# Windowed attention in six layers on one core: the roots of Q move from GpSimd's products into ScalarE's exponentials, in 64-key pieces

## The reference

```
q = l2norm(q) * qs;  k = l2norm(k) * ksc
q = q * cos * scale + rotate_half(q) * sin * scale
k = k * cos / scale + rotate_half(k) * sin / scale
sim = einsum('bhwie,bhwje->bhwij', bq, bk2) * 8      # 32 queries, 64 keys
sim = where(mask, -max, sim)                         # a key is visible 32 back
out = einsum('bhwij,bhwje->bhwie', softmax(sim, -1), bv2)
x = x + out @ Wo
x = x + (a * gelu(gate)) @ W2 + b2                   # a, gate = norm(x) @ W1 + b1
```

## Time and profile before

| | us |
|---|---|
| median of three runs | 4397.81 (4393.16 to 4399.85) |
| profiled execution | 4392.85 |
| its span, first to last instruction | 4391.0 |
| TensorE matmuls, busy | 3735.3 (85%) |
| VectorE busy | 2756.5 (63%) |
| GpSimd busy | 2491.9 (57%) |
| ScalarE busy | 1823.6 (42%) |
| mean granted clock of TensorE | 0.934 of full |

### The profile page before, as it was taken

The page is one execution under the profiler, slowest core; times in us unless marked ns, Lnnn a source line. Parts: engine busy times, 40 slices in busy tenths (PEclk is TensorE's granted clock), DMA queues, the critical chain, the costliest instruction groups (busy, mean ns, idle before and its releaser), DMA issues.

```text
span 4391.0 us, 146256 instructions
## 1 busy us (share of the span) xinstructions
PE 3735.3 (85%) x65128; PEld 2403.2 (55%) x65320; DVE 2756.5 (63%) x3583; ACT 1823.6 (42%) x2989; POOL 2491.9 (57%) x1948
## 2 busy tenths in 40 slices
PE   8999986788888888888888888888888888888887
PEld 4444443455555555556555555555555555555554
DVE  4544553666666666667677666666766666666662
ACT  4545553333443434344344343434344434343333
POOL 0000001866677766767667676666766667666651
PEclk9999997898999999999999999998999999999897
DMA  1000001544444444444444444444444444444331
GB/s 43 6 6 6 8 3 34 160 134 128 134 139 141 138 132 127 144 133 146 132 137 143 129 138 134 131 132 130 150 131 138 129 128 134 138 132 138 125 115 41
DMA packets 222595, 490.18 MB, mean 112 GB/s; under 512 B 63759, under 2 KB 101901, under 8 KB 221837
## 3 DMA queue, kind: packets, MB, share of 16 engines
q1 hardware_dynamic: 196080, 465.08, 33.8%
q10 hardware_dynamic: 25884, 15.73, 1.3%
HBM read 224.80 MB, written 7.34 MB: 53 GB/s over the span
## 4 chain that ended last, share of the span: by engine, by line
PE 52%; DVE 13%; issue 13%; POOL 9%; ACT 8%; DMA 3%; SPq 1%; ACTq 0%; DVEq 0%; POOLq 0%
PE PS L518 52%; ACT AOT L1235 2%; POOL SC L1338 2%; DVE TPB L924 2%; ACT SX L1212 2%; POOL Q L1315 2%; DVE MX L950 2%; POOL K L1315 2%; DVE PX L970 1%; ACT SC L1229 1%; DMA TR<-TPB 1%; DVE SC L952 1%; DMA PP<-PX 1%; POOL Q L1333 1%; DVE PP L969 1%
## 5 line engine op out<-in xcount | busy, mean ns | idle before, releaser
L924 DVE SCALAR_TENSOR_TENSOR TPB<-PS,VEC,C 128x1024 f32<-128x1024 f32 x768 | 977.7, 1282 | 590.8 <-ACT SX L1212 555.1
L518 PE MATMUL PS<-PP,VV 32*64 32x64 f32 (+1 forms) x24576 | 572.0, 229 | 253.7 <-ACT AOT L1235 149.0
L518 PEld LDWEIGHTS PS<-PP,VV 32*64 32x64 f32 x24576 | 461.6, 138 | 528.4 <-issue 484.5
L1338 POOL TENSOR_TENSOR SC<-SC,RC 128x1024 f32<-128x1024 f32 x192 | 365.7, 1904 | 543.7 <-DVE RC L961 543.7
L1315 POOL TENSOR_TENSOR Q<-Q,RB 128x512 f32<-128x512 f32 x384 | 491.2, 1279 | 134.9 <-DMA RB<-root_scratch 134.1
L1212 ACT ACTIVATE SX<-PS 128x512 f32<-128x512 f32 x768 | 460.5, 601 | 233.1 <-PE PS L518 227.8
L1333 POOL TENSOR_TENSOR Q<-TPB,TR 128x512 f32<-128x512 f32 x384 | 489.5, 1275 | 118.1 <-DMA TR<-TPB 103.4
L1315 POOL TENSOR_TENSOR K<-K,RB 128x512 f32<-128x512 f32 x384 | 491.3, 1280 | 0.0
L1333 POOL TENSOR_TENSOR K<-TPB,TR 128x512 f32<-128x512 f32 x384 | 490.0, 1276 | 0.0
L1225 ACT COPY VV<-PS 128x512 f32<-128x512 f32 x384 | 223.2, 581 | 625.4 <-PE PS L518 575.6
L518 PE MATMUL PS<-LXH,LH 128*128 128x512 f32 x768 | 362.3, 472 | 13.2 <-POOL LL L1309 8.0
(11 more groups left out here) (164 smaller groups left out, 6644.9 us busy)
## 6 DMA issues: line engine op xcount, KB each, us to landing
TR<-TPB SPq DMA_DIRECT2D x768, 256.0 KB
RB<-root_scratch SPq DMA_DIRECT2D x768, 256.0 KB, 4.1
PP<-PX SPq DMA_DIRECT2D x192, 192.0 KB, 3.0
WS<-in_wqkv ACTq DMA_DIRECT2D x72, 128.0 KB, 2.5
PP<-PX SPq DMA_DIRECT2D x192, 48.0 KB, 4.0
root_scratch<-NV SPq DMA_DIRECT2D x384, 8.0 KB
LO<-in_wo ACTq DMA_DIRECT2D x6, 512.0 KB, 5.2
T<-in_x SPq DMA_DIRECT2D x8, 256.0 KB, 3.1
```

Source lines behind the costliest of these rows:

```text
L518: return e.matmul(dst, lhsT, rhs, start=start, stop=stop, **kw)
L924: e.scalar_tensor_tensor(TPB[:, n % 3:4 + n % 2:3 + n % 2 - n % 3, w, :], g, VEC[:, l, 9 + w:10 + w], C[:, at:at + 1024].rearrange("p (o c ...
L1338: e.tensor_tensor(sc, sc, RC[m % 2][:, :].rearrange("p (g o) -> p g o", o=1).broadcast_to([128, 16, 64]), ALU.mult).then_inc(sem["np_pool" ...
```

## The change

The roots of Q are no longer multiplied into Q. The scores in banks 0 and 1 so lack a factor for each query and head, and ScalarE applies it: exp(r * score - r * MX), with r from a small tile RQ as scale and -MX * r from a small tile BQ as bias. Both are one number per partition, so one exponential covers one group of 64 keys, 16 of them for a pair, straight from PSUM. The subtraction on VectorE goes; a product of 128x16 makes BQ. RQ, once in four rounds, is a transpose on TensorE of NV and a copy on ScalarE. The selection matrix tsel orders the rows so that the 8 roots of Q come first. RB holds K's roots only, and GpSimd's PR is one product a round in place of two. S1 on TensorE now waits for the exponentials of the pair before (they read the banks).

Stages move as well: S3 in two halves, the first ahead of VP, the second behind PVn; SU to the end of the even round, GpSimd's product by RC (now stage NP) ahead in the odd round, TT as before at its end; in odd rounds PV 0 behind SS; F3 into the middle of k = 6 with GpSimd's part (F3l) at its end; the feed-forward products in three parts over k = 7; GpSimd's parts of WC and W1 (WL, W1l) at the end of their rounds, with LW two rounds later.

```diff
-            part("tsel")[64 * s:64 * s + 64, 32 * i + 4 * (i // 2) + 2 * s + i % 2] = 1.0
+            part("tsel")[64 * s:64 * s + 64, 32 * i + 8 * (i % 2) + 4 * (i // 4) + 2 * s + i // 2 % 2] = 1.0
...
+    def feed(u, i):
+        group("F4g", 3 * u + i, "f4_act", 3 * u + i + 1)
+        group("F4a", 3 * u + i, "f4_dve", 3 * u + i + 1)
...
+        late = k == 7 and 0 <= u - 1 < NB * DEPTH
         if even and scores:
             o.put("S1", m)
-        if values:
-            o.put("PV", p, 2 if even else 0)
+        if late:
+            o.put("TB", u - 1, 0)
+            feed(u - 1, 0)
+        if even and values:
+            o.put("PV", p, 2)
         if ss:
             o.put("SS", 2 * n + 14)
             o.put("SS", 2 * n + 15)
+        if not even and values:
+            o.put("PV", p, 0)
         if n % 4 == 0 and 0 <= n + 4 < NS:
             o.put("NM1", (n + 4) // 4)
+        if n % 4 == 1 and 0 <= n + 3 < NS:
+            group("RQ", (n + 3) // 4, "rq_act", (n + 3) // 4 + 1)
         if 0 <= n + 3 < NS:
             o.put("RB", n + 3)
         if 0 <= n + 2 < NS:
-            o.put("PR", 2 * n + 4)
-            o.put("PR", 2 * n + 5)
+            o.put("PR", n + 2)
+        if even and scores:
+            o.put("S3", m, 0)
         if not even and scores:
-            o.put("SU", m)
+            o.put("NP", m)
+        if late:
+            feed(u - 1, 1)
...
+        if k == 6 and 0 <= u - 1 < NB * DEPTH:
+            group("F3", u - 1, "f3_dve", u)
         if 0 <= n + 8 < NS:
             group("PJ", 2 * n + 16, "pj_dve", 2 * n + 17)
-        if even and scores:
-            o.put("S3", m)
         if values:
             o.put("PV", p, 3 if even else 1)
             if even:
                 o.put("PVn", p)
+        if even and scores:
+            o.put("S3", m, 1)
         if n % 4 == 0 and 0 <= n + 4 < NS:
             o.put("NM2", (n + 4) // 4)
+        if late:
+            feed(u - 1, 2)
+            o.put("TB", u - 1, 1)
         if 0 <= n + 8 < NS:
             group("PJ", 2 * n + 17, "pj_dve", 2 * n + 18)
-        if not even and scores:
-            o.put("TT", m)
+        if scores:
+            o.put("SU" if even else "TT", m)
...
                 elif st == "S1":
                     m, = key
                     if m:
-                        on.wait_ge("s1_dve", 2 * m)
+                        on.wait_ge("s3_act", 2 * m)
...
-                    e.tensor_tensor(sc, g, MX[:, :].rearrange("p (g o) -> p g o", o=1).broadcast_to([128, 16, 64]),
-                                    ALU.subtract).then_inc(sem["s1_dve"], 1)
+                    if m > 1:
+                        on.wait_ge("s3_act", 2 * m - 2)
+                    on.wait_ge("rq_act", m // 2 + 1)
+                    e.scalar_tensor_tensor(BQ[m % 2][:, :], MX[:, :], -1.0, rq(m), ALU.mult, ALU.mult).then_inc(sem["s1_dve"], 1)
...
                 elif st == "S3":
-                    m, = key
+                    m, s = key
+                    r = rq(m)
+                    if m:
+                        on.wait_ge("tt_dve", 2 * m)
+                    on.wait_ge("rq_act", m // 2 + 1)
                     on.wait_ge("s1_dve", 2 * m + 2)
-                    e.activation(SC[:, :, :, :], SC[:, :, :, :], ACT.Exp).then_inc(sem["s3_act"], 1)
+                    for i in range(8):
+                        g = 8 * s + i
+                        p = e.activation(SC[:, g, :, :].rearrange("p x k -> p (x k)"), bank[s][:, 64 * i:64 * i + 64], ACT.Exp,
+                                         bias=BQ[m % 2][:, g:g + 1], scale=r[:, g:g + 1])
+                    p.then_inc(sem["s3_act"], 1)
...
                 elif st == "PR":
-                    i, = key
-                    dst = (Q, K)[i % 2][:, i // 2 % 8, :]
-                    on.wait_ge("ad_pool", i + 1)
-                    on.wait_ge(f"rb_in{i // 2 % 2}", 32 * (i // 4) + 32)
-                    e.tensor_tensor(dst, dst, RB[i // 2 % 2][:, i % 2, :], ALU.mult).then_inc(sem["pr_pool"], 1)
+                    n, = key
+                    dst = K[:, n % 8, :]
+                    on.wait_ge("ad_pool", 2 * n + 2)
+                    on.wait_ge(f"rb_in{n % 2}", 32 * (n // 2) + 32)
+                    e.tensor_tensor(dst, dst, RB[n % 2][:, :], ALU.mult).then_inc(sem["pr_pool"], 1)
```

More of the change, by code:

```diff
@@ L246, in do, with tail @@
         turn.setdefault(n, []).append(lambda: f(*a))
+    last = {}
+    def tail(n, f, *a):
+        last.setdefault(n, []).append(lambda: f(*a))
     for l in range(DEPTH):
@@ L256, in order @@
             do(at[c], o.put, "WC", 12 * l + c)
+            if l:
+                tail(at[c], o.put, "WL", 12 * l + c)
+            else:
+                do(at[c], o.put, "WL", c)
             if c < 9:
-                do(at[c], o.put, "LW", 12 * l + c + 3)
-        do(first + 1, o.put, "L1", l)
-        do(first + 3, group, "WB", l, "wb_dve", l + 1)
+                do(at[c] + 2 * (l > 0), o.put, "LW", 12 * l + c + 3)
+        do(first + 2, o.put, "L1", l)
+        do(first + 4, group, "WB", l, "wb_dve", l + 1)
         do(first + 9, o.put, "W1", l)
+        tail(first + 9, o.put, "W1l", l)
         do(first + 4 if l else -9, o.put, "LO", l)
@@ L309, in order @@
             o.put("AD", 2 * n + 15)
+        for f in last.get(n, ()):
+            f()
+        if k == 6 and 0 <= u - 1 < NB * DEPTH:
+            o.put("F3l", u - 1)
         fill(u - 1, k)
@@ L383, in build @@
         MX = sb("MX", [128, 16])
+        BQ = [sb(f"BQ{i}", [128, 16]) for i in range(2)]
+        RQ = [sb(f"RQ{i}", [128, 2, 16]) for i in range(2)]
         SM = sb("SM", [128, 16])
@@ L386, in build @@
         NV = sb("NV", [128, 3, 128])
-        RB = [sb(f"RB{i}", [128, 2, L]) for i in range(2)]
+        RB = [sb(f"RB{i}", [128, L]) for i in range(2)]
         XCH = sb("XCH", [128, L], F32R)
@@ L438, in lb, with rq @@
             return u // NB, u % NB
+        def rq(m):
+            return RQ[m // 2 % 2][:, m % 2, :]
         def xready(u):
@@ L710, in tensor_program @@
                     p.then_inc(sem["s1_pe"], 1)
+                elif st == "RQ":
+                    q, = key
+                    on.wait_ge("nm_dve", 4 * q + 4)
+                    free(on, st, key)
+                    e.transpose(bk(st, key)[:, 0:128], NV[:, 2, :], ident).then_inc(sem["rq_pe"], 1)
                 elif st == "PV":
@@ L1226, in scalar_program @@
                 elif st == "S3":
-                    m, = key
-                    on.wait_ge("s1_dve", 2 * m + 2)
-                    e.activation(SC[:, :, :, :], SC[:, :, :, :], ACT.Exp).then_inc(sem["s3_act"], 1)
+                    m, s = key
[3 more added lines that the diff above has]
+                    on.wait_ge("rq_act", m // 2 + 1)
+                    on.wait_ge("s1_dve", 2 * m + 2)
+                    for i in range(8):
[3 more added lines that the diff above has]
+                    p.then_inc(sem["s3_act"], 1)
+                elif st == "RQ":
+                    q, = key
+                    on.wait_ge("rq_pe", q + 1)
+                    e.copy(RQ[q % 2][:, :, :].rearrange("p y (i c) -> p (y i) c", c=4),
+                           bk(st, key)[:, 0:128].rearrange("p (c i) -> p i c", c=4)[:, 0:8, :]).then_inc(sem["rq_act"], 1)
                 elif st == "PVn":
```

24 lines of the change are left out of this document (12 added, 12 removed).

## The result

The changed kernel takes 4990.32 us (median of four runs, 4982.56 to 4991.67) against 4398.83 for the kernel before beside it. The ratio is 1.1337, 95% interval 1.1311 to 1.1363: slower by 13%, some 590 us. The forecast was 4980. The profiled execution has a span of 4980.8 us.

What follows compares the result with a forecast made beforehand. No engine is full; a cycle of waits over each pair of rounds sets the time. 80.0 + 5.2 = 85.2 us a batch against 72.9, over 48 batches, adds 590 to 4393: 4980 us, range 4600 to 5280.

Steps and rivals of the forecast that it cites:

- The cycle, the central step: In a pair of rounds: both halves of the pieces lie on the cycle, 16.4 us where 12.0 stood.
- The piece: On ScalarE: each exponential of 64 columns with two operand tiles follows the last after 0.31 us, bounds 0.14 and 0.43.
- Rivals A and B: ScalarE's pieces: A, operands free, 0.14 us each, 4210 us, 12%; B, only one operand charged, 4730 us, 20%.
- The wait at SS: TensorE's second SS waits for the square of K behind the second eight pieces; TensorE idles 6.3 us a pair.
- The clock: TensorE's clock falls to 1.2 GHz after idling: 1.3 us a pair, 5.2 a batch, bounds 0 and 2.6 a pair.
- Rival C: On TensorE: each pair runs its whole odd round at 1.2 GHz, 90.4 us a batch, 5230 us; chance 15%.
- Pair by pair: Cycle by pair of rounds from k = 0: 18.2, 21.9, 18.5 and 21.4 us, sum 80.0 a batch against 69.4.
- F5 on TensorE is now hidden: In k = 0, 1: F5's products cost nothing, but VectorE's two additions, 1.5 us, make the pair 18.2 us.
- RQ, which I put at nothing: In k = 0, 1: the new transpose takes 0.3 us; its wait for NM2's last step was put at nothing.
- The relief of GpSimd: GpSimd's 384 products of Q leave, 491 us; a plain pair from 12.1 to 9.6; real only if it ends last.
- the split of F4: In k = 6, 7: the feed-forward split wins, with no stall of 3 us, and lies beside the waits.
- the product with V behind SS: TensorE's odd rounds: moving this product behind SS costs 0.6 us and would be free in the old order.

Runs made afterwards that it cites:

- e1: Changed kernel with the second eight exponential pieces moved behind the square of K in ScalarE's queue: 4665.12 us.
- e2: Changed kernel with its 16 pieces a pair kept, but no bias and a constant scale in place of the tiles BQ and RQ: 4420.72 us.
- e11: Changed kernel with its pieces and the bias tile BQ kept, but a constant scale in place of RQ: 4667.11 us.
- e3: Changed kernel with one exponential of 128x1024 in place of the 16 pieces, at the first half's place, without row maxima and roots of Q: 4312.12 us.
- e9: Changed kernel with 19 idle bf16 products on TensorE ahead of the second SS's wait in rounds k = 3 and 5: 4833.57 us.
- e7: Kernel before the change with GpSimd's product of Q by its roots left out, all transfers kept: 4303.38 us.
- e6: Kernel before the change with only the moves of the feed-forward part and of the weights: 4365.01 us.
- e4: Changed kernel with the product with V of the odd rounds put back ahead of SS: 4966.32 us.

## Why the prediction was right, point by point

- *The cycle, the central step.* 80.0 us a batch before the clock. e1 shows that the order on ScalarE counts, for 325 of 592 us with the load the same; e2, e11 and e3 show that the length of the pieces counts too, nearly one for one when the clock that comes back with it is included. The path was right.
- *The piece.* 0.31 us forecast from the Gelu row and the short logarithm, 0.293 measured; 0.438 the median length of one (0.424 forecast). The operand price, 0.087 from one row, is 0.094 to 0.096. The overlap is 0.15 (0.438 less 0.293) and not 0.11, so a somewhat longer piece came out somewhat closer to the next. Rivals A and B (free operands) fall: neither operand is free.
- *The wait at SS.* The second SS waits for the square of K, as said. I had the idle time at 6.3 us in each pair; in the pair shown it is two waits, 1.11 and 3.35, so 4.5, and on average over the loop 432.1/192 = 2.3, or 3.3 with the waits for VV. In k = 0, 4, 6 and 7 other products of TensorE fill a part. MX started 2437.46, the square was ready 8.7 us behind it (9.1 forecast), but TensorE's even round ended 3.7 behind it and not 2.7, and the first SS lies between the waits.
- *The clock.* 5.2 us a batch, taken as half of 2.6 in each of four pairs. e9 gives back 157 us, 3.3 a batch: 1.9 in k = 2 and 3, 0.9 in k = 4 and 5, 0.6 in k = 0 and 1. So the term is real and was spread wrongly. k = 6, 7 hardly has it, since the feed-forward products cover the wait (0.4 us a batch is left of it). What the low clock costs behind the waits for VV and X, no run tells. Rival C (every odd round wholly at 1.2 GHz) falls with 85.2 us a batch in place of 90.4, though k = 3 comes near to it, with 2.2 of its 2.6 us.
- *Pair by pair.* With the clock's share I had 19.5, 23.2, 19.8 and 22.7; the medians are 20.7, 23.8, 20.0 and 21.2. The sum of 85.2 equals the measured mean, but in part by errors that cancel. The step that failed is "F5 on TensorE is now hidden, but its two additions on VectorE stand before TPB and make it 18.2": I counted them in VectorE's queue and overlooked the bank. The product of Q in the odd round (PJ 2n+16) needs the bank that F5 holds until the additions are done, 77.8 us of TensorE's waits (1.6 us a batch). In the batch shown the granted clock was 0.50 in the 4 us behind it (2430 to 2434). RQ, which I put at nothing, has a part in it: by order() it takes the first bank of the ring in k = 1, so that F5's bank comes round to the product of Q and no longer to that of K. The two causes were not tested apart. Against that k = 6, 7 was 1.5 us shorter. That 4980 came so near to 4990 is luck to that extent.
- *The relief of GpSimd.* "That is real only while GpSimd ends last": e7 gives 91 us of 491.
- *The moves.* The saying that here "the split of F4 wins" held, but its price was not weighed: e6 is worth 29 us only, since XCL is needed sooner. That the product with V behind SS "costs 0.6 of that and would be free in the old order" left out the next bank: e4 gained at most 24 us of the 115, as TPB held it.

## What to carry to other kernels

Splitting one instruction to get a per-group operand costs the fixed price of each piece plus the price of each operand tile, and on an engine that is 40% busy it can still cost one for one: ask where the instruction stands in its queue and which square, copy or sum behind it the busiest engine is waiting for. Work taken off an engine that seldom ends last gives back little: here a fifth of itself, 91 of 491 us. When a stage is moved, look for the bank or buffer it holds until its last consumer, and for what its first instruction needs at the new place.

## What the runs showed of the hardware

Short ScalarE instructions in a row overlap more than long ones: exponentials of 64 columns from PSUM follow each other at 0.103 us with constant scale and bias, 0.196 with one operand tile, 0.293 with two. Their median lengths are 0.287, 0.356 and 0.438, so they overlap by 0.15 to 0.18, where the rows before gave 0.11 for 512 and 1024 columns. And useless matmuls can pay: 19 of them, 3.2 us, ahead of a wait made the kernel 157 us faster, and TensorE's granted clock was 1.00 in the 4 us behind the wait shown, where it had been 0.50 for the first 3. 24 in the same place, which overran the square, took 1.5 us off k = 2 and 3 in place of 1.9, and 16 where nothing waited added 2.4.
